# A routed feed-forward kernel: x loaded turned for the router, and the matrices of conditioning by one gather

## The chip, the cores and the metric

One core of a Trainium2 chip runs the whole program. TensorE (PE) multiplies, VectorE (DVE) and ScalarE (ACT) work on its results, GpSimd (POOL) issues the gathers and scatters that go by a list of rows, and SyncE (SP) issues the other DMAs. The metric is device microseconds for one execution; less is better.

## The reference, cut to what matters

```python
w = weights[conditions]                      # 32 of 200 matrices, 64 x 64
xf = einsum('bct,bcd->bdt', x, w)            # x: 32 x 64 x 512; conditioning
logits = einsum('nh,eh->ne', xf, Wr)         # 2048 tokens, 8 experts
gate = softmax(logits); top2 = top_k(gate, 2)
rank = (cumsum(onehot) * onehot).sum(-1); keep = rank <= 640
y = sum over the two experts of gate * Wd(silu(Wg xf) * (Wu xf))
return x + y
```

## The kernel before

The 32 samples are 16 tiles of 128 rows of x (two samples of 64 channels each), eight pairs of tiles in all. Logits don't wait for conditioning: the router's weights are applied to x itself, and each sample's small result is then multiplied by that sample's 64 x 64 matrix (`logits`). For this TensorE turns each tile of x (`x_tile_turn`, L1176), ACT or DVE copies the turned tile out of PSUM (`turn_copy` L810 and L600), `router` (L1188) multiplies it, and `turn` (L1199) turns its small result back. `condition` (L1232) multiplies x by the matrices, two tiles at a time in a ring of four PSUM banks; ACT copies every result (`xf_copy`, L592) and SP stores it to `xf_dram` (L390, L394), from where experts gather their tokens.

The matrices reach `wq` in two ways: tiles 0 to 7 by one row gather each on POOL (L453), tiles 8 to 15 by one gather into `wsel_sb` (L446) and eight placing DMAs of 32 KB on SP's queue (L361), which turn 16 partitions of whole pieces into 128 partitions of rows.

After the logits DVE finds the top two, `oh` is filled, TensorE counts ranks (L1267, L1270), DVE works out the slot of every token (L901 to L929), TensorE makes the lists from it (L1281), and DVE writes `src_row` (L950). POOL then gathers the first expert's tokens into `xg` (L507), for which it waits for `src_row` and for all stores of `xf_dram`. Meanwhile TensorE runs `KEEP_WARM` multiplications whose result nobody reads (L1287). The first use of `xg` is the turn at L1301; from there on the experts run one after the other.

Each engine's order is the order of the code of its block, and an instruction that waits holds all those behind it on its engine. The DMAs of SP start in SP's order. `raw` is the buffer of an expert's weights (five units: four of gate and up, one of down), `w` their split into a high part (ACT, `w_high`) and a low part (DVE, `w0_low`).

Of the kernel before, what the change touches and what calls it, by code (L numbers as in the profile page):

```python
# [22 lines left out]
PLACED = B // 2  # L23
CQ = P // PLACED
# [15 lines left out]
BEFORE_RANKS = 4  # L40
W0_EARLY = 1
LG = ((0, 3), (3, 5), (5, 7), (7, NM))
GATED = 2 * LG[1][1]
EARLY_PAIRS = 2
WARM_UP = 10

KEEP_WARM = 18
# [24 lines left out]
def build(nc, x, cond, wcond, wr, wgu, wd, out):  # L72
# [12 lines left out]
    with ctx:  # L85
# [25 lines left out]
        condb = sb("condb", [P, HALF + 1], I32)  # L111
        row_i = sb("row_i", [P, 1], I32)
        part_i = sb("part_i", [P, 2], I32)
        part = sb("part", [P, 2])
        cidx = sb("cidx", [P, HALF + 1], U32)
# [68 lines left out]
        ps_tT = ps_xf = bank[0:XR]  # L184
# [20 lines left out]
        row_in = [sem(f"row_in{g}") for g in range(len(LG) - 1)]  # L205
        placed = [sem(f"placed{g}") for g in range(1, len(LG))]
        tT_ps = sem("tT_ps")
        tT_act_ok = sem("tT_act_ok")
        tT_dve_ok = sem("tT_dve_ok")
# [69 lines left out]
        TURN_DVE = [1, 2, 5, 6, 9]  # L279
        TURN_ACT = [j for j in range(TT) if j not in TURN_DVE]  # L280

# [61 lines left out]
        def _(sp):  # L343

            def load_x(m):

                js = slice(m * 2, m * 2 + 2)
                sp.dma_start(x_sb[:, js, :], x_t[:, js, :]).then_inc(x_in[m], 16)

            sp.dma_start(condb[:, :], cond[:, :]).then_inc(cond_in, 16)  # L350
            load_x(0)
            load_x(1)
            sp.dma_start(wr_sb[:, :, :], wr[:, :, :]).then_inc(wr_in, 16)
            for m in range(2, NM):
                load_x(m)
# [3 lines left out]
            def place(j):  # L359

                sp.dma_start(wq[:, j, :], wsel_sb[(j - HALF) * 2 * CQ:(j - HALF + 1) * 2 * CQ, :]  # L361
                             .rearrange("q (c d) -> q c d", d=D)).then_inc(placed[group_of(j) - 1], 16)

            sp.wait_ge(wsel_in, 16)
            for j in range(HALF, TT):
                place(j)
# [25 lines left out]
            for j in range(TT - 2, TT):  # L392
                sp.wait_ge(xf_ok, j + 1)
                sp.dma_start(xf_t[:, j:j + 1, :], xf_sb[:, j:j + 1, :]).then_inc(xf_out, 16)  # L394
            sp.wait_ge(gates_ok, 2)
# [39 lines left out]
        def _(pool):  # L435
# [9 lines left out]
            pool.wait_ge(cidx_ok, 2)  # L445
# [3 lines left out]
                in_offset=bass.IndirectOffsetOnAxis(ap=cidx[:, HALF:HALF + 1], axis=0),  # L449
            ).then_inc(wsel_in, 16)  # L450

            for j in range(HALF):
                nc.gpsimd.indirect_dma_start(  # L453
                    out=wq[:, j, :], out_offset=None, in_=wcond[:, :],
                    in_offset=bass.IndirectOffsetOnAxis(ap=cidx[:, j:j + 1], axis=0),
                ).then_inc(row_in[group_of(j)], 16)
# [28 lines left out]
            pool.wait_ge(xf_out, 16 * (TT // 2 + 2))  # L485
# [102 lines left out]
        def _(act):  # L588
            def xf_copy(n, s):

                act.wait_ge(xf_ps, n + 1)
                nc.scalar.activation(xf_sb[:, bass.ds(n, 1), 0:H], ps_xf[s][:, :].unsqueeze(1),  # L592
                                     ACT.Copy).then_inc(xf_ok, 1)

            for j in TURN_ACT:
                act.wait_ge(tT_ps, j + 1)
                if j >= XR:
                    act.wait_ge(xrT_ps, j // 2 - 1)
                nc.scalar.activation(turned_sb[:, j % XR, :, :],  # L600
                                     ps_tT[j % XR][:, :].rearrange("p (k c) -> p k c", k=KH),
                                     ACT.Copy).then_inc(tT_act_ok, 1)
# [12 lines left out]
            def exps(h):  # L615

                act.wait_ge(sub_ok, (1, 3)[h])
                js = (slice(0, GATED), slice(GATED, TT))[h]
                nc.scalar.activation(ex[:, js, :], lg[:, js, :], ACT.Exp).then_inc(ex_ok, 1)

            for n in range(2):
                xf_copy(n, n)
            exps(0)
            for n in range(2, XR):
                xf_copy(n, n)
            for u in range(W0_EARLY):
                w_high(u, 0, 0)
            for n in range(XR, XR + 2):
                xf_copy(n, n - XR)
            exps(1)  # L630
            for n in range(XR + 2, 2 * XR):
                xf_copy(n, n - XR)
            with act.Fori(2, TT // XR) as i:
                for s in range(XR):
                    xf_copy(i * XR + s, s)

            for u in range(W0_EARLY, KH):
                w_high(u, 0, 0)
# [121 lines left out]

            act.wait_ge(consts, IDENT)
            nc.scalar.activation(g_sb[:, 0:1], ident[:, 0:1], ACT.Silu).then_inc(silu_warm, 1)
            w_high(KH, 0, 0)
            x_high(0)
            act.wait_ge(silu_warm, 1)
            act.wait_ge(more_ok, 1)
# [807 lines left out]
```

## Time and profile before

| what | us |
|---|---|
| median of 3 runs (272.05 to 273.76) | 272.7 |
| the profiled execution | 271.69 |
| its span, first to last instruction | 270.0 |
| first turn of a gathered token tile (L1301) starts | 41.62 |
| last `xf_copy` ends | 33.17 |

The span leaves out 1.7 us of the profiled execution. All that the change touches lies ahead of 41.62 us and in the first expert; the other seven experts take the rest of the span. Start times below are from the span's start. An issue of a DMA is shown as an instruction of its queue (SPq, POOL); the landing is given apart.

### The profile page before, as it was taken

The numbers are of one execution on the slowest core, as the hardware profiler recorded it, in microseconds if no ns is written. First come the engines' busy times: TensorE is split into PE (matmuls) and PEld (weight loads), VectorE is DVE, ScalarE is ACT, GpSimd is POOL, SyncE is SP. The second block draws the span as 40 slices with busy tenths as digits, with TensorE's granted clock in tenths as the row PEclk, the third lists the DMA queues.
The fourth block names the chain that finished last, engine by engine and source line by source line (L and its number), as shares of the span: only waits on it lengthen the run. The fifth ranks groups of instructions, "written<-read, shape, count | busy, mean of one in ns | idle before, by whom it ended". The sixth has DMA issues, their size and how long they took to land.

```text
span 270.0 us, 4016 instructions
## 1 busy us (share of the span) xinstructions
PE 257.5 (95%) x1368; PEld 199.9 (74%) x1368; DVE 161.8 (60%) x332; ACT 137.6 (51%) x242; POOL 171.2 (63%) x156
## 2 busy tenths in 40 slices
PE   8999798999999999999999999999999999999991
PEld 4563257999987867888878877887878777778980
DVE  2558997544459674776556638656773967243251
ACT  2356861444464655665376644666475368442100
POOL 5792047731158858875788387768876885585742
PEclk9999979999999999999999999999999999999998
DMA  6999848998879997899789867997899799366541
GB/s 203 364 305 342 358 165 266 382 330 312 298 221 214 203 253 197 138 253 276 178 143 231 245 189 124 241 322 174 171 266 298 127 182 216 41 79 81 146 164 45
DMA packets 27099, 59.00 MB, mean 219 GB/s; under 512 B 6198, under 2 KB 6454, under 8 KB 26976
## 3 DMA queue, kind: packets, MB, share of 16 engines
q1 hardware_dynamic: 16416, 37.89, 44.3%
q0 software_dynamic: 10656, 20.75, 37.2%
q8 instruction: 16, 0.26, 0.4%
q14 instruction: 11, 0.09, 0.1%
HBM read 39.56 MB, written 20.25 MB: 222 GB/s over the span
## 4 chain that ended last, share of the span: by engine, by line
PE 55%; DVE 18%; DMA 9%; ACT 8%; issue 6%; SPq 1%; ACTq 1%; POOLq 0%; DVEq 0%
PE bank L1340 16%; PE bank L1427 10%; PE bank L1314 10%; DMA xg<-xf_dram,src_turn 6%; PE bank L1435 5%; DVE w L996 4%; DVE squares L1045 4%; ACT hhi L695 3%; DMA x_sb<-x 3%; PE bank L1287 2%; PE bank L1301 2%; PE bank L1176 2%; DVE xlo L981 2%; ACT w L608 2%; DVE h L1111 1%
## 5 line engine op out<-in xcount | busy, mean ns | idle before, releaser
L1427 PE MATMUL bank<-xhi,w 128*128 128x512 f32 x280 | 71.5, 397 | 0.2 <-DVE h_last L1091 0.2
L1340 PE MATMUL bank<-w,hhi 128*128 128x512 f32 (+1 forms) x216 | 67.1, 392 | 1.1 <-DVE hlo L1051 1.1
L553 POOL DMA_INDIRECT out<-y_sb,dst_row x35 | 56.1, 1604 | 14.8 <-issue 10.4
L1427 PEld LDWEIGHTS bank<-xhi,w 128*128 128x128 f32 x280 | 52.5, 188 | 13.2 <-DVE h_last L1091 0.7
L519 POOL DMA_INDIRECT gate_g<-gates_dram,src_row x40 | 45.2, 1130 | 12.1 <-issue 10.5
L1340 PEld LDWEIGHTS bank<-w,hhi 128*128 128x128 f32 x216 | 39.2, 188 | 10.2 <-DVE hlo L1051 2.3
L996 DVE TENSOR_TENSOR w<-raw,w 128x704 fp32r<-128x704 f32 (+1 forms) x35 | 37.0, 1058 | 14.6 <-ACT w L608 8.2
L1340 PE MATMUL bank<-w,hlo 128*128 128x512 f32 (+1 forms) x108 | 42.0, 389 | 0.0
L507 POOL DMA_INDIRECT xg<-xf_dram,src_turn x24 | 25.5, 1063 | 26.1 <-DVE xlo L981 11.7
L1435 PE MATMUL bank<-xlo,w 128*128 128x512 f32 x140 | 38.4, 396 | 0.0
L608 ACT ACTIVATE w<-raw 128x704 fp32r<-128x704 f32 (+1 forms) x40 | 36.7, 922 | 0.0
L507 POOL DMA_INDIRECT xg<-xf_dram,src_row x16 | 17.6, 1102 | 27.9 <-DVE dst_row L965 15.7
L1045 DVE STREAM_TRANSPOSE squares<-xg 128x512 f32<-128x512 f32 x24 | 24.0, 1051 | 16.7 <-DMA xg<-xf_dram,src_turn 16.7
L1435 PEld LDWEIGHTS bank<-xlo,w 128*128 128x128 f32 x140 | 26.4, 188 | 6.4
L666 ACT ACTIVATE y_sb<-bank,gate_g 128x512 f32<-128x512 f32 x30 | 20.1, 685 | 20.0 <-PE bank L1340 18.7
L1340 PEld LDWEIGHTS bank<-w,hlo 128*128 128x128 f32 x108 | 20.3, 188 | 4.7
L1314 PE MATMUL bank<-w,xhi 128*128 128x352 f32 x112 | 20.5, 328 | 0.8 <-ACT xhi L643 0.8
L1314 PEld LDWEIGHTS bank<-w,xhi 128*128 128x128 f32 x112 | 18.2, 189 | 1.5 <-issue 1.0
L695 ACT ACTIVATE hhi<-h 128x512 fp32r<-128x512 f32 x14 | 8.8, 632 | 19.5 <-DVE h L1098 12.0
L1051 DVE TENSOR_TENSOR hlo<-h,hhi 128x512 fp32r<-128x512 f32 x14 | 9.7, 696 | 10.4 <-ACT hhi L695 10.4
L981 DVE TENSOR_TENSOR xlo<-xg,xhi 128x512 fp32r<-128x512 f32 x24 | 15.0, 685 | 0.2 <-ACT xhi L653 0.2
L653 ACT ACTIVATE xhi<-xg 128x512 fp32r<-128x512 f32 x24 | 13.2, 617 | 1.5 <-DMA xg<-squares 1.5
(138 smaller groups left out, 304.3 us busy)
## 6 DMA issues: line engine op xcount, KB each, us to landing
raw<-wgu SPq DMA_DIRECT2D x32, 352.0 KB, 7.7
xg<-squares SPq DMA_DIRECT2D x24, 256.0 KB, 7.1
x_sb<-x SPq DMA_DIRECT2D x8, 512.0 KB, 8.3
raw<-wd SPq DMA_DIRECT2D x8, 512.0 KB
xf_dram<-xf_sb SPq DMA_DIRECT2D x7, 512.0 KB, 3.7
raw<-wd SPq DMA_DIRECT2D x8, 192.0 KB
out<-x SPq DMA_DIRECT2D x1, 1280.0 KB, 17.9
gate_g<-gates_dram,src_row POOLq DMA_INDIRECT x40, 4.5
```

The source lines that it names most:

```text
L507: nc.gpsimd.indirect_dma_start(out=xg[:, t, :], out_offset=None, in_=xf_dram[:, :], in_offset=bass.IndirectOffsetOnAxis(ap=rows, axis=0), ...
L519: nc.gpsimd.indirect_dma_start(out=gate_g[:, n % TPE, :], out_offset=None, in_=gates_dram[:, :], in_offset=bass.IndirectOffsetOnAxis(ap=sr ...
L553: nc.gpsimd.indirect_dma_start(out=out[:, :], in_=y_sb[:, n % TPE, :], in_offset=None, out_offset=bass.IndirectOffsetOnAxis(ap=dst_row[:, ...
L608: last = nc.scalar.activation(w[:, half, 0, a:b], raw[:, a:b], ACT.Copy)
L666: nc.scalar.activation(y_sb[:, t, :], y_bank(e, t)[:, :], ACT.Copy, scale=gate_g[:, t, e:e + 1]).then_inc(y_ok, n)
L981: nc.vector.tensor_tensor(xlo4[:, :, cols], turned_rows(e, t), xhi4[:, :, cols].bitcast(F32), ALU.subtract).then_inc(xlo_ok, n)
L996: last = nc.vector.tensor_tensor(w[:, half, 1, a:b], raw[:, a:b], w[:, half, 0, a:b].bitcast(F32), ALU.subtract)
L1045: nc.vector.transpose(squares[:, :, t, :], xg[:, t, :].rearrange("p (i b) -> p b i", i=SQ)).then_inc(squares_ok, 1)
L1314: last = nc.tensor.matmul(ps[:, 0:I], left[:, b, c], w[:, half, part, o:o + I], start=(k == 0 and left is xhi and part == 0), stop=(k == K ...
L1340: last = nc.tensor.matmul(ps[:, cols], left(c), w[:, half, part, o:o + width], start=(c == 0 and q == 0), stop=(closes and c == cs[-1] and ...
L1427: last = nc.tensor.matmul(ACC_BANK[what][:, :], columns(what, k, part), xhi4[:, k, :], start=(k == 0 and part == 0), stop=False)
L1435: last = nc.tensor.matmul(ACC_BANK[what][:, :], columns(what, k, 0), xlo4[:, k, :], start=False, stop=(k == KH - 1))
```

## The change

Outside the kernel a second copy of x, `xt`, is made in which every pair of tiles is turned. SP loads it into the place of x (`x_sb`), 4 KB for a partition where rows were two pieces of 2 KB. `router` reads it at once: 16 tile turns and their 16 copies on ACT and DVE are gone. Conditioning needs the rows: for pairs 0, 1 and 2 SP loads them over the turned ones, once the router has read these (`load_x_rows`); for pairs 3 to 7 TensorE turns the tiles back (`turn_rows`) and ACT copies them to `x_sb` (`rows_copy`). Pairs are conditioned in the order 3, 4, 0, 1, 2, 5, 6, 7, with two places in the ring. One gather of 128 rows of 4 KB now fetches all 32 matrices, and ACT issues 16 placing DMAs, each from 8 partitions, ahead of all its other work. Exponentials and gates are worked out once for all tiles and no longer in two parts. Units 2 to 4 of the first expert's weights are loaded after the stores of `xf_dram`; `x_low(0)` now stands ahead of `w0_low(KH)`; `KEEP_WARM` goes from 18 to 28.

```diff
-PLACED = B // 2
-CQ = P // PLACED
+CQ = P // B
-W0_EARLY = 1
+W0_EARLY = 2
+ROWS_LOADED = (0, 1, 2)
+ROWS_TURNED = (3, 4, 5, 6, 7)
+CONDITIONED = (3, 4, 0, 1, 2, 5, 6, 7)
-KEEP_WARM = 18
+KEEP_WARM = 28
 SP:
+            def load_x_turned(m):
+                sp.dma_start(x_sb[:, m * 2:m * 2 + 2, :], xt[m, :, :, :]).then_inc(x_in[m], 16)
+            def load_x_rows(n):
+                m = ROWS_LOADED[n]
+                sp.wait_ge(xrT_ps, m + 1)
+                sp.dma_start(x_sb[:, js, :], x_t[:, js, :]).then_inc(rows_in[n], 16)
-            sp.wait_ge(wsel_in, 16)
-            for j in range(HALF, TT):
-                place(j)
+            for n in range(len(ROWS_LOADED)):
+                load_x_rows(n)
...
-            for u in range(NU):
+            for u in range(W0_EARLY):
                 load_unit(0, u)
-            for m in range(NM - 1):
-                sp.wait_ge(xf_ok, m * 2 + 2)
+            for n, m in enumerate(CONDITIONED):
+                sp.wait_ge(xf_ok, n * 2 + 2)
...
+            for u in range(W0_EARLY, NU):
+                load_unit(0, u)
 POOL:
-            for j in range(HALF):
-                nc.gpsimd.indirect_dma_start(
-                    out=wq[:, j, :], out_offset=None, in_=wcond[:, :],
...
 ACT:
+            act.wait_ge(wsel_in, 16)
+            for j in range(TT):
+                act.dma_start(wq[:, j, :], wsel_sb[j * 2 * CQ:(j + 1) * 2 * CQ, :]
+                              .rearrange("q (c d) -> q c d", d=D)).then_inc(placed[group_of(j)], 16)
+            def rows_copy(m, ring):
+                for o in range(2):
+                    act.wait_ge(turned_ps, ROWS_TURNED.index(m) * 2 + o + 1)
+                    nc.scalar.activation(x_sb[:, m * 2 + o, :], ps_xf[ring * 2 + o][:, :],
+                                         ACT.Copy).then_inc(turned_ok, 1)
 PE:
-            def x_tile_turn(j):
...
+            def turn_rows(m, ring):
+                for o in range(2):
+                    for k in range(KH):
+                        last = nc.tensor.transpose(ps_xf[ring * 2 + o][:, k * P:(k + 1) * P],
+                                                   xt_sb[:, m * 2 + o, k, :], ident[:, :])
+                    last.then_inc(turned_ps, 1)
+            def condition(m, ring):
...
+                if m in ROWS_LOADED:
+                    pe.wait_ge(rows_in[ROWS_LOADED.index(m)], 16)
+                else:
+                    pe.wait_ge(turned_ok, ROWS_TURNED.index(m) * 2 + 2)
```

On ACT, from its first instruction: before, it loads its table, copies turned tiles and then results of conditioning (`xf_sb`).

```order
L600 ACT_TABLE_LOAD
L600 ACTIVATE turned_sb<-bank 128x512 [waits tT_ps] x2
L600 ACTIVATE turned_sb<-bank 128x512 [waits xrT_ps,tT_ps] x9
L592 ACTIVATE xf_sb<-bank 128x512 [waits xf_ps] x2
L619 ACTIVATE ex<-lg 128x80 [waits sub_ok]
L592 ACTIVATE xf_sb<-bank 128x512 [waits xf_ps] x2
L608 ACTIVATE w<-raw 128x704 [waits raw_in0]
```

On ACT from its first instruction in the changed kernel (`x_sb` are the rows turned back; `wsel_in` counts the landed gather):

```order
L577 DMA wq<-xf_sb 128x1x64 [waits wsel_in]
L577 DMA wq<-xf_sb 128x1x64 x15
L591 ACT_TABLE_LOAD
L591 ACTIVATE x_sb<-bank 128x512 [waits turned_ps] x4
L584 ACTIVATE xf_sb<-bank 128x512 [waits xf_ps]
L584 ACTIVATE xf_sb<-bank 128x512
L584 ACTIVATE xf_sb<-bank 128x512 [waits xf_ps]
L584 ACTIVATE xf_sb<-bank 128x512
L591 ACTIVATE x_sb<-bank 128x512 [waits turned_ps] x4
```

The sixteen placings, the wait for the gather ahead of them and the table load behind them now stand before every copy.

On TensorE around the last router step, before: L1221 are logits, L1232 conditioning, L1188 the router, L1199 its turn, L1267 and L1270 the ranks.

```order
L1221 MATMUL bank_5<-xr,wq 64x8 x8
L1232 MATMUL bank<-x_sb,wq 64x512 x4
L1188 MATMUL bank_7<-turned_sb,wr_sb 32x256 x4
L1199 MATMUL bank_7<-ident,xrT 128x128 x2
L1232 MATMUL bank<-x_sb,wq 64x512 x4
L1199 MATMUL bank_7<-ident,xrT 128x128 x2
L1221 MATMUL bank_5<-xr,wq 64x8 x8
L1221 MATMUL bank_7<-xr,wq 64x8 x4
L1232 MATMUL bank<-x_sb,wq 64x512 x8
L1267 MATMUL bank_7<-ohp,ones 128x264
```

The same place of TensorE in the changed kernel (L1167 logits, L1182 conditioning, L1130 the router, L1150 its turn, L1140 turning rows back, L1220 the ranks):

```order
L1167 MATMUL bank_5<-xr,wq 64x8 x8
L1182 MATMUL bank<-x_sb,wq 64x512 x4
L1130 MATMUL bank_7<-x_sb,wr_sb 32x256 x4
L1150 MATMUL bank_7<-ident,xrT 128x128 x4
L1167 MATMUL bank_5<-xr,wq 64x8 x8
L1167 MATMUL bank_7<-xr,wq 64x8 x4
L1182 MATMUL bank<-x_sb,wq 64x512 x4
L1140 MATMUL bank<-ident,x_sb 128x128 x16
L1220 MATMUL bank_7<-ohp,ones 128x264
```

The first conditioning, of pair 3, still stands ahead of the last router step, but now it waits for ACT's copies of the rows; two pairs of tiles are turned back ahead of the ranks.

## Rows read from the trace of the kernel before

**Rows 1.** The chain that ended last, in order of time: start us, us, what

```profile
33.43 2.55 PE bank L1281 x32
35.98 5.58 PE bank L1287 x18
...
41.62 0.64 PE bank L1301 x4
```

**Rows 2.** Timeline of POOL, then the landing of DMAs issued from 37 to 39

```profile
37.46 1.55 POOL L507 DMA_INDIRECT xg<-xf_dram,src_row  x1 [15.70 <-DVE dst_row L965]
...
xg<-xf_dram,src_row POOLq DMA_INDIRECT x1, 4.0
```

**Rows 3.** Timeline of SP and its DMA issues from 0 to 50: KB, median us to landing

```profile
10.87 5.14 SPq L361 DMA_DIRECT2D wq<-xf_sb  x8
...
32.71 1.32 SPq L394 DMA_DIRECT2D xf_dram<-xf_sb  x2
...
xf_dram<-xf_sb SPq DMA_DIRECT2D x7, 512.0 KB, 3.7
...
xf_dram<-xf_sb SPq DMA_DIRECT2D x2, 256.0 KB, 3.4
```

**Rows 4.** Timeline of DVE, 34.9 to 50.5

```profile
36.02 0.20 DVE L950 TENSOR_SCALAR src_row<-bank 128x40 uint32<-128x40 f32 x1
...
43.52 3.58 DVE L1144 COPY src_turn<-src_row 32x6 uint32<-32x6 uint32 x16
47.14 0.69 DVE L974 TENSOR_TENSOR xlo<-bank,xhi 128x512 fp32r<-128x512 f32 x1
```

**Rows 5.** Timeline of ACT, 20 to 52

```profile
24.75 0.79 ACT L608 ACTIVATE w<-raw 128x704 fp32r<-128x704 f32 x1
...
26.86 1.09 ACT L592 ACTIVATE xf_sb<-bank 128x512 f32<-128x512 f32 x2
...
31.11 2.06 ACT L592 ACTIVATE xf_sb<-bank 128x512 f32 x4 [0.32 <-PE bank L1232]
...
35.24 1.28 ACT L762 ACT_TABLE_LOAD   x1
```

**Rows 6.** The gathering queue, 8 to 9 and 9 to 10 us: packets, MB, share

```profile
q0 software_dynamic: 21, 0.09, 23.6%
...
q0 software_dynamic: 71, 0.19, 50.9%
```

**Rows 7.** Timeline of TensorE, 18 to 30, and one step of the first expert

```profile
18.47 1.09 PE L1176 MATMUL bank<-ident,x_sb 128*128 128x128 f32 x8
...
20.69 1.07 PE L1232 MATMUL bank<-x_sb,wq 64*64 64x512 f32 x8
21.69 0.64 PE L1188 MATMUL bank<-turned_sb,wr_sb 128*32 128x256 f32 x8
...
24.01 0.78 PE L1221 MATMUL bank<-xr,wq 64*64 64x8 f32 x24
...
48.71 0.80 PE L1314 MATMUL bank<-w,xlo 128*128 128x352 f32 x4
```

**Rows 8.** Stretches: busy us (instructions) of PE, PEld, DVE, ACT, POOL; PEclk, DMA share, GB/s

```profile
30.00:33.40 3.40, 1.93 (x16) 0.27 (x13) 3.23 (x10) 3.08 (x7) 0.00 (x0) 1.00 0.90 361
...
36.00:39.40 3.40, 3.40 (x9) 1.18 (x8) 3.27 (x11) 2.10 (x3) 1.64 (x2) 0.50 0.08 22
39.40:41.60 2.20, 2.16 (x10) 0.79 (x9) 2.00 (x2) 0.00 (x0) 1.90 (x2) 1.00 0.54 145
```

**Rows 9.** By tile (raw) and line: ns min/median/max of one, first and last start us

```profile
L372 SPq DMA_DIRECT2D raw<-wgu x8: 333/432/587, 16.1 to 42.9; - x8
...
L941 DVE TENSOR_TENSOR w<-raw,w x5: 873/885/1753, 35.1 to 39.6; 128x704 fp32r<-128x704 f32 x4, 128x1536 fp32r<-128x1536 f32 x1
```

**Rows 10.** DMAs issued from 43 to 43.5, and packets from 15.9 to 18.2

```profile
xg<-xf_dram,src_row POOLq DMA_INDIRECT x1, 7.0
...
DMA packets 1323, 0.48 MB, mean 209 GB/s; under 512 B 1232, under 2 KB 1232, under 8 KB 1323
```

More of the change, by code:

```diff
@@ L204, in build @@
         wsel_in = sem("wsel_in")
[L205 to L209, printed above, removed]
+        placed = [sem(f"placed{g}") for g in range(len(LG))]
+        rows_in = [sem(f"rows_in{m}") for m in ROWS_LOADED]
+        turned_ps = sem("turned_ps")
+        turned_ok = sem("turned_ok")
         xrT_ps = sem("xrT_ps")
@@ L613, in w_high, with exps @@
                 last.then_inc(whi_ok, 1)
[L615 to L637, printed above, removed]
+            def exps():
+                act.wait_ge(sub_ok, 2)
+                nc.scalar.activation(ex[:, :, :], lg[:, :, :], ACT.Exp).then_inc(ex_ok, 1)
+            rows_copy(3, 0)
+            rows_copy(4, 1)
+            xf_copy(3, 0)
+            xf_copy(4, 1)
+            rows_copy(5, 0)
+            rows_copy(6, 1)
+            xf_copy(0, 0)
+            xf_copy(1, 1)
+            rows_copy(7, 0)
+            xf_copy(2, 1)
+            exps()
+            xf_copy(5, 0)
+            xf_copy(6, 1)
+            w_high(0, 0, 0)
+            xf_copy(7, 0)
+            for u in range(1, KH):
                 w_high(u, 0, 0)
@@ L942, in w0_low @@
                                         ALU.subtract).then_inc(wlo0_ok, 1)
-            for u in range(W0_EARLY):
-                w0_low(u)
+            gates()
             dve.wait_ge(slot_ps, 1)
@@ L966, in _ @@
                                     ALU.add).then_inc(lists_ok, 1)
-            for u in range(W0_EARLY, KH):
+            for u in range(KH):
                 w0_low(u)
@@ L1240, in _ @@
             pe.wait_ge(consts, IDENT)
-            for m in range(NM):
-                x_tile_turn(m * 2)
-                x_tile_turn(m * 2 + 1)
-                if m == 1:
-                    pe.wait_ge(wr_in, 16)
-                if m >= 1:
-                    router(m - 1)
-                if m >= 2:
-                    turn(m - 2)
-                if m in (6, 7):
-                    logits(m - 6)
-            condition(0)
+            pe.wait_ge(wr_in, 16)
+            for m in range(NM - 1):
+                router(m)
+                if m >= 1:
+                    turn(m - 1)
+                if m == 3:
+                    turn_rows(3, 0)
+                if m == 4:
+                    turn_rows(4, 1)
+                if m in (5, 6):
+                    logits(m - 5)
+            pe.wait_ge(turned_ok, 2)
+            condition(3, 0)
             router(NM - 1)
             turn(NM - 2)
-            condition(2)
             turn(NM - 1)
@@ L1258, in _ @@
             logits(3)
-            after = EARLY_PAIRS * 2 + BEFORE_RANKS
-            for j in range(EARLY_PAIRS * 2, after, 2):
-                condition(j)
+            pe.wait_ge(turned_ok, 4)
+            condition(4, 1)
+            pe.wait_ge(xf_ok, 2)
+            turn_rows(5, 0)
+            pe.wait_ge(xf_ok, 4)
+            turn_rows(6, 1)
             pe.wait_ge(consts, RANKS)
@@ L1272, in _ @@
             last.then_inc(rank_ps, 1)
-            for j in range(after, TT, 2):
-                condition(j)
+            pe.wait_ge(turned_ok, 6)
+            condition(0, 0)
+            pe.wait_ge(turned_ok, 8)
+            condition(1, 1)
+            pe.wait_ge(xf_ok, 6)
+            turn_rows(7, 0)
+            pe.wait_ge(xf_ok, 8)
+            condition(2, 1)
+            pe.wait_ge(turned_ok, 10)
+            condition(5, 0)
+            pe.wait_ge(xf_ok, 10)
+            condition(6, 1)
+            pe.wait_ge(xf_ok, 12)
+            condition(7, 0)
             pe.wait_ge(consts, CONSTS)
```

164 lines of the change are left out of this document (52 added, 112 removed).

## The prediction

> **What bounds the kernel now.** I read the chain of waits first, up to the first turn of a gathered tile. It runs through the multiplication that makes the lists, through 18 fillers, and into that turn at 41.62 [rows 1]. The fillers hide two things that end together. One is on POOL: the gather into `xg` is issued at 37.46 and lands 4.0 us later, at 41.5 [rows 2], while the fillers end at 41.56. So the turn waits for the gather, and I asked what the gather waits for. `src_row` is there at 36.2 [rows 4]; the last two stores of `xf_dram` are issued from 32.7 to 34.0 and land 3.4 us after their issue starts, so the later one at about 37 [rows 3]. The list is ready more than 1 us before the gather starts: the stores set the start, and behind them stands ACT, whose last copy of a result ends at 33.17 [rows 5]. From this copy to the turn it takes 8.4 us. So the question for the change is when ACT makes its last copy, and whether the lists stay ahead of it.
>
> **What goes away.** Sixteen tile turns on TensorE and sixteen copies, and on POOL eight row gathers, on SP eight placings (5.14 us) [rows 3]. All of this lies ahead of the last router step at 21.69 [rows 7], and it is worth only as much as that step and the conditioning behind it come sooner. In the changed order neither can: conditioning of pair 3 stands ahead of the last router step on TensorE and waits for ACT's copies of the rows.
>
> **When ACT begins.** ACT's first instruction waits for the gather of the matrices. Before, SP began to place at 10.87, when a gather of 256 KB had landed [rows 3]; its queue moved little until 9 us and then 0.19 MB in a microsecond, half of the DMA engines [rows 6]. Twice the bytes at that rate take 1.4 us more: 12.2. Bounds are 10.5 (nothing more, indices a little earlier) and 14.4 (bytes and competition both double the stretch from 8.6). Then sixteen issues. The trace has none on ACT. The nearest row is the same transfer of 32 KB on SP's queue, 5.14 us for eight, 0.643 each [rows 3]; the shortest DMA issue of its kind is 0.333 [rows 9]. I take SP's: 10.3 us, ACT is through at 22.5. The lower bound is 5.0 us less. Then ACT loads its table, 1.28 us [rows 5], which before was hidden at the start: 23.8.
>
> **ACT's work from there.** It has 26 copies in place of 16: ten of rows, sixteen of results, at 0.545 us (two in 1.09), 14.2 us; one exponential, 0.27; the high part of weight unit 0 ahead of the last pair, 0.79 [rows 5]. That is 15.2. To this come waits. Rows of pair 3 are copied at 24.9, TensorE conditions it by 25.95 (1.07) [rows 7], and then does the last router step, its turns and the logits. Before, that took 3.1 us from 21.69 to 24.79 with one conditioning in between, which covered 0.4 us of DVE's work; without it, 2.4 [rows 7]. So logits end at 28.4 and pair 4 is conditioned at 29.4, while ACT had finished pair 3 at 27.1: it waits 2.3 us. Pair 0 comes after two pairs are turned back (1.06 each, 1.09 in the row) [rows 7] and after the ranks: ACT waits another 0.5. After that ACT doesn't wait. 23.8 + 15.2 + 2.9, with 0.1 of hops, is 42.0 for the last copy, against 33.17.
>
> **From the last copy to the turn.** The last store, now 512 KB, lands 3.6 us after its issue (median 3.7) [rows 3]: 45.6. A gather of 4.0 [rows 2] from 45.7 lands at 49.7. But units 2 to 4 of the weights, 1.4 MB, now stand right behind the last store on SP's queue. A gather beside such loads took 7.0 instead of 4.0 [rows 10]; this one meets only their end, and I add 1.0 (bounds 0 and 3): 50.7. TensorE's side: the lists come after the last conditioning, at 40.1, and end at 42.65 (2.55) [rows 1]. Eighteen fillers took 5.6 us, nine of them in 3.4 us at a granted 0.50, which is 1.2 GHz, the others at 0.216 each at full clock [rows 8]; ten more are 2.2, so 28 end at 50.5. The turn starts at 50.7, 9.1 later than before. The late units themselves are off the path: units 2 and 3, 0.7 MB right behind a store that lands at 45.6, land at 48 to 49 at the rate of that store, and ACT's and DVE's parts of them (0.79 and 0.88) [rows 5, 9] end before the second half of the first expert's first step needs them. If that cover goes, it costs up to 1 us.
>
> **The clock.** The granted clock fell to 0.50 at 36 after a stretch in which TensorE was busy 1.93 of 3.4 us, and stayed there for 3.4 us of fillers [rows 8]. While ACT places, TensorE has nothing but a few small logits from about 17 to 25, so I expect the low clock when pair 3 begins. Its conditioning, the router step, turns and logits, 3.1 us of work on the path, would then take up to 1.7 us more. I take 0.8.
>
> **DVE in the first expert.** `x_low(0)` now comes ahead of `w0_low(KH)`, which can start only when ACT has made the high part behind its first copy, and the sixteen copies of `src_turn` stand behind that. From the turn: 2.8 us until the high part is there, 1.75 [rows 9], 3.58 [rows 4], so the second `xlo` starts after 8.15 and ends after 8.85, where before it started after 5.5 (47.14) [rows 4]. TensorE needs it 7.1 us after the turn (48.71) [rows 7]. So 1.75 us of a new stall, and nothing hides it.
>
> **The sum.** 9.1 + 0.8 + 1.75 = 11.65 us on the profiled execution's 271.7, that is 283.3. The median of the runs lies 1.0 above that execution, so I forecast 284.3, given as 284. The POOL time set free, exponentials and gates in one piece (counted with ACT, or beside waiting on DVE) and 4 KB pieces for x are worth nothing: none is on this path.
>
> **Rivals.** (1) *ACT's issues are short.* If one holds ACT only 0.333 us [rows 9], everything from ACT's start comes 5.0 us sooner: 279.3. For it: some loads on SP are issued in as little. Against: the same transfer took 0.592 at the least on SP, which the eight in 5.14 us bear out. (2) *The placings run on half of the engines.* Before, a placing read 16 partitions and now it reads 8. In the trace 1232 small packets took most of 2.3 us [rows 10], so the 1024 of eight placings some 1.9. If the number of source partitions sets the number of engines, twice the packets on half of the engines occupy these for 7.6 us; with half of their time [rows 6] the last matrix lands about 28, just when logits want it; with a third, about 35, 7 us late. The middle costs 3.5 to 4 us, since logits stand ahead of all other conditioning on TensorE: 288. It decides from a landing after 28.4. The trace can't speak for it, since no placing of before reads fewer than 16 partitions. The Trainium skill has this as a rule (DMA: Bandwidth & Descriptors, section "Why a DMA increments its semaphore by 16 and not by 1"): a DMA is spread over the largest number of engines, up to 16, that divides the slowest dimension of both of its sides, which would be 8 here; no run here shows it. (3) *Not slower.* The last copy would have to end at 33.17 less the 1.75 of DVE's stall. ACT's work and waits behind the table load are 18.2 us, so that load would have to end by 13.2, and the gather land and sixteen issues pass by 11.9. That needs the gather at about 10.5 and issues that hold ACT hardly at all (0.1 us each, under any row). For it: ACT is shown issuing nothing, so its price isn't known. Then the last copy comes at 33.5, the weights' 1.0 falls away with the wait, and the time is 272 to 274.
>
> **How the numbers follow.** The forecast gets 0.70, (1) 0.12, (2) 0.11, (3) 0.07. The low end of the range joins both low bounds of ACT's start (5.0 and 1.7): 284.3 - 6.7, 278. The high end: the gather at 14.4 (2.2), the full 7.0 of the token gather (2.0), the whole clock loss (0.9): 289.4, which holds (2) as well. A measurement of this kernel can tell about 1%, 2.7 us. Of (3) I count 0.05 as within 1% and 0.02 as faster; all other cases are slower by over 1%.
>
> **What would show it.** In the changed profile: sixteen placings on ACT's queue of about 0.64 us each from about 12.2, then a table load and the first copy to `x_sb` near 24; the last conditioning copy near 42; the first `xg` gather near 46; the turn near 51 to 52; a second `xlo` 8 us behind the turn. A first copy before 18 would make me wrong by rival (1); logits that wait for the placings after 28, by (2).

## The result, and the profile after

The changed kernel takes 289.3 us (median; 287.6 to 292.1), the kernel before 273.2 on the same chip: a ratio of 1.0574, with a 95% interval of 1.0505 to 1.0642. It is slower, as forecast, 5 us beyond the forecast of 284 and just inside the range, whose upper end is 289.4. Ratios (not medians) leave out executions more than 1.5% above the fastest of the same kernel, and the profiled executions of "old matrices", "38 fillers", "both" and "rows on DVE" are such ones, so for these I read where waits stand rather than the total, and "both", with one execution left, has no ratio.

The profiled execution took 287.6 us, the least of the four, 15.9 more than that of before. First the chain of waits of the changed kernel, from the last placings to the first turn of a gathered tile (start us, us, what):

```profile
24.68 0.61 ACTq L577
...
25.32 1.28 ACT L591
26.61 1.09 ACT x_sb L591 x2
...
27.84 1.99 PE bank L1182 x8
29.83 1.05 PE bank L1130 x8
...
32.79 0.96 PE bank L1182 x8
...
33.78 1.10 ACT xf_sb L584 x2
...
44.81 0.98 ACT xf_sb L584 x2
45.81 2.97 DMA xf_dram<-xf_sb
...
49.55 5.07 DMA xg<-xf_dram,src_row
...
54.76 1.06 PE bank L1266 x4
```

Before, this stretch of the chain was TensorE's lists and fillers up to a turn at 41.62 [rows 1]. Now it begins with ACT's DMA issues, goes through its table load and its first copies of rows, the conditioning of pair 3, the last router step and, by turns, ACT's copies and TensorE's turning and conditioning to the last store, and ends in a turn at 54.76, 13.1 us later. ACT, on its own timeline, places, and much later makes its last copy of a result, which ends at 45.78 in place of 33.17 [rows 5]:

```profile
12.82 12.47 ACTq L577 DMA_DIRECT2D wq<-xf_sb  x16
...
33.78 1.09 ACT L584 ACTIVATE xf_sb<-bank 128x512 f32<-128x512 f32 x2 [2.81 <-PE bank L1182]
...
44.69 1.09 ACT L584 ACTIVATE xf_sb<-bank 128x512 f32<-128x512 f32 x2
```

TensorE's timeline shows who else waits for the placings (first line), that the fillers end at 52.72, 2.03 us before the turn, and what follows from this in the first expert:

```profile
23.66 0.53 PE L1167 MATMUL bank<-xr,wq 64*64 64x8 f32 x24 [4.53 <-DMA wq<-xf_sb]
...
46.50 6.22 PE L1252 MATMUL bank<-iota_q 128*128 128x512 f16 x28
54.76 1.04 PE L1266 MATMUL bank<-ident,xg 128*128 128x128 f32 x4 [2.03 <-DMA xg<-xf_dram,src_row]
56.58 2.69 PE L1279 MATMUL bank<-w,xhi 128*128 128x352 f32 x8 [0.78 <-ACT xhi L631]
...
64.58 0.81 PE L1279 MATMUL bank<-w,xlo 128*128 128x352 f32 x4
65.23 0.49 PE L1333 MATMUL bank<-ident,h_sb 128*128 128x128 f32 x3
```

The stretches of the same execution (busy us of PE, PEld, DVE, ACT and POOL; then the granted clock, DMA share and GB/s) tell why eight multiplications take 2.69 us, where the same eight took 1.53 before: the clock is at 0.50, which is 1.2 GHz, after the wait of 2.03 us. It is there from 25 to 30 as well, after the wait of 4.53:

```profile
25.00:30.00 5.00, 3.59 (x34) 1.37 (x34) 2.39 (x25) 3.46 (x6) 0.00 (x0) 0.50 0.11 17
30.00:35.00 5.00, 4.35 (x53) 2.09 (x46) 3.29 (x25) 2.19 (x5) 0.00 (x0) 0.91 0.26 107
...
55.00:60.00 5.00, 4.22 (x16) 3.85 (x15) 2.82 (x5) 1.97 (x2) 4.24 (x4) 0.50 0.88 293
```

From the turn to the first turn of h (line 1333) it took 10.47 us; in the trace before it took 7.73. So the 15.9 us are 13.14 up to the turn and 2.74 behind it; the rest of the kernel adds nothing. DVE's timeline answers to [rows 4]:

```profile
57.84 1.76 DVE L906 TENSOR_TENSOR w<-raw,w 128x1536 fp32r<-128x1536 f32 x1 [0.68 <-ACT w L598]
59.52 3.39 DVE L1106 COPY src_turn<-src_row 32x6 uint32<-32x6 uint32 x16
62.94 0.69 DVE L936 TENSOR_TENSOR xlo<-bank,xhi 128x512 fp32r<-128x512 f32 x1
```

The second `xlo` starts 8.18 us behind the turn, forecast as 8.15. Yet TensorE reaches its use only at 64.58, when `xlo` has been there since 63.6: after half clock TensorE is later than DVE here.

Last, the queues. q1 is SP's, q10 ACT's placings. From 17 to 21 and from 22 to 24 us (packets, MB, share of 16 engines):

```profile
q1 hardware_dynamic: 703, 1.45, 97.3%
q10 hardware_dynamic: 336, 0.08, 9.4%
...
q10 hardware_dynamic: 1029, 0.25, 57.0%
q1 hardware_dynamic: 19, 0.04, 6.4%
```

While SP's queue still loads rows and weights, the placings get 84 packets of 256 bytes in a microsecond; once it is through they get 514, and then 57% of the engines' time.

### The profile page after: what moved, and what is told of

It reads as the page before. It is cut to its first block, busy times and chain, and to the rows that moved or that the text cites. A ratio compares the mean times of both kernels' runs of the same rounds, so it can differ in the third digit from the quotient of the medians.

```text
span 285.9 us, 3939 instructions
## 1 busy us (share of the span) xinstructions
PE 264.0 (92%) x1354; PEld 202.3 (71%) x1354; DVE 158.1 (55%) x321; ACT 136.4 (48%) x240; POOL 168.0 (59%) x148
## 4 chain that ended last, share of the span: by engine, by line
PE 59%; DMA 14%; DVE 9%; ACT 6%; ACTq 4%; issue 4%; SPq 1%; POOL 1%; POOLq 1%; DVEq 0%
PE bank L1305 18%; PE bank L1394 15%; PE bank L1279 10%; PE bank L1402 7%; ACTq L577 4%; DMA xg<-xf_dram,src_turn 4%; DMA xf_sb<-wcond,cidx 3%; DMA xg<-squares 3%; DVE w L958 3%; DVE squares L1007 3%; PE bank L1182 2%; PE bank L1266 2%; ACT xf_sb L584 2%; DMA xg<-xf_dram,src_row 2%; PE bank L1409 1%
## 5 line engine op out<-in xcount | busy, mean ns | idle before, releaser
L539 POOL DMA_INDIRECT out<-y_sb,dst_row x35 | 57.4, 1640 | 14.6 <-issue 10.4
L505 POOL DMA_INDIRECT gate_g<-gates_dram,src_row x40 | 48.0, 1200 | 12.1 <-issue 11.2
L493 POOL DMA_INDIRECT xg<-xf_dram,src_turn x24 | 26.0, 1082 | 24.6 <-DVE xlo L943 9.9
L654 ACT ACTIVATE y_sb<-bank,gate_g 128x512 f32<-128x512 f32 x30 | 20.2, 686 | 20.0 <-PE bank L1305 18.6
L1279 PE MATMUL bank<-w,xhi 128*128 128x352 f32 x112 | 22.0, 344 | 0.8 <-ACT xhi L631 0.8
L1279 PEld LDWEIGHTS bank<-w,xhi 128*128 128x128 f32 x112 | 19.6, 202 | 1.6 <-issue 1.1
L1013 DVE TENSOR_TENSOR hlo<-h,hhi 128x512 fp32r<-128x512 f32 x14 | 9.7, 692 | 10.4 <-ACT hhi L683 10.4
```

The lines of the kernel that those rows point to most:

```text
L493: nc.gpsimd.indirect_dma_start(out=xg[:, t, :], out_offset=None, in_=xf_dram[:, :], in_offset=bass.IndirectOffsetOnAxis(ap=rows, axis=0), ...
L505: nc.gpsimd.indirect_dma_start(out=gate_g[:, n % TPE, :], out_offset=None, in_=gates_dram[:, :], in_offset=bass.IndirectOffsetOnAxis(ap=sr ...
L539: nc.gpsimd.indirect_dma_start(out=out[:, :], in_=y_sb[:, n % TPE, :], in_offset=None, out_offset=bass.IndirectOffsetOnAxis(ap=dst_row[:, ...
L654: nc.scalar.activation(y_sb[:, t, :], y_bank(e, t)[:, :], ACT.Copy, scale=gate_g[:, t, e:e + 1]).then_inc(y_ok, n)
L1279: last = nc.tensor.matmul(ps[:, 0:I], left[:, b, c], w[:, half, part, o:o + I], start=(k == 0 and left is xhi and part == 0), stop=(k == K ...
```

## The experiments

Each is the changed kernel with one edit. Ratios are to the kernel before on the same chip. The last four columns are of the profiled execution (us): ACT's first copy, the end of the last copy of a result, the first turn of a gathered tile, and from there to the turn of h.

| kernel | median | ratio to before | first copy | last copy ends | turn | to turn of h |
|---|---|---|---|---|---|---|
| before | 272.6 to 273.2, by chip | 1 | | 33.17 | 41.62 | 7.73 |
| after | 289.3 | 1.0574 [1.0505, 1.0642] | 26.61 | 45.78 | 54.76 | 10.47 |
| placings on SP | 282.0 | 1.0327 [1.0273, 1.0381] | 13.84 | 38.09 | 48.35 | 9.28 |
| rows after placing | 286.9 | 1.0526 [1.0490, 1.0563] | 25.02 | 47.23 | 56.51 | 9.27 |
| sixteen partitions | 286.1 | 1.0517 [1.0426, 1.0608] | 22.73 | 44.37 | 52.48 | 9.27 |
| table first | 290.6 | 1.0636 [1.0570, 1.0703] | 26.24 | 47.08 | 56.07 | 10.43 |
| rows on DVE | 289.4 | 1.0521 [1.0433, 1.0609] | 29.62 | 48.40 | 57.81 | 9.26 |
| list early | 289.2 | 1.0626 [1.0540, 1.0712] | 26.68 | 47.48 | 55.63 | 9.21 |
| 38 fillers | 289.2 | 1.0583 [1.0517, 1.0649] | 27.50 | 48.53 | 57.91 | 9.27 |
| both | 289.6 | none | 27.53 | 48.74 | 57.71 | 7.79 |
| clock held | 291.0 | 1.0633 [1.0544, 1.0722] | 27.36 | 47.52 | 56.97 | 10.45 |
| old matrices | 281.4 | 1.0259 [1.0183, 1.0334] | 12.29 | 40.22 | 49.06 | 9.30 |
| old matrices, mended | 279.3 | 1.0236 [1.0193, 1.0278] | 13.17 | 40.63 | 49.44 | 7.73 |
| on SP, mended | 280.6 | 1.0320 [1.0266, 1.0375] | 14.71 | 38.36 | 48.95 | 7.74 |

**Placings on SP.** The five lines move from ACT to SP, ahead of the loads of rows:

```diff
 # sync
+            sp.wait_ge(wsel_in, 16)
+            for j in range(TT):
+                sp.dma_start(wq[:, j, :], wsel_sb[...]...).then_inc(placed[group_of(j)], 16)
             for n in range(len(ROWS_LOADED)):
                 load_x_rows(n)
 # scalar
-            act.wait_ge(wsel_in, 16)
-            for j in range(TT):
-                act.dma_start(wq[:, j, :], wsel_sb[...]...).then_inc(placed[group_of(j)], 16)
```

> The changed kernel with its 16 placings issued by SP, ahead of the row loads, in place of ACT. Theory (ACT is held by the wait for the gather, 16 issues and a table load, 12.8 to 26.6): the table load falls back to the start, ACT copies the rows of pair 3 by 17, and conditioning of pair 3 waits only for the matrices, about 22.5 in place of 27.84; logits end at 26 to 27 in place of 32.8; the last copy comes near 41 in place of 45.8, the first turn near 50 in place of 54.76; the time is 4 to 5.5 us under the changed kernel's, a ratio to the kernel before of 1.037 to 1.043. Rival A (ACT's 26 copies and the ring of two places are the cost, not its late start): last copy within 1.5 of 45.8, ratio 1.052 or more. Rival B (placings from 8 partitions run on half of the engines and are what the logits wait for): logits still end after 30.

The direction is the theory's, and the gain is larger than it forecast: pair 3 is conditioned at 21.1, logits end at 25.1, and the ratio of 1.0327 lies below the expected 1.037 to 1.043, which its interval just reaches. Neither rival's sign shows: the last copy is 7.7 us earlier, and the logits end well before 30. SP's timeline, then ACT's and POOL's:

```profile
12.44 10.42 SPq L361 DMA_DIRECT2D wq<-xf_sb  x16
...
13.84 0.60 ACT L591 ACTIVATE x_sb<-bank 128x512 f32<-128x512 f32 x1 [11.74 <-PE bank L1140]
...
44.08 1.00 POOL L498 DMA_INDIRECT xg<-xf_dram,src_row  x1 [32.25 <-DMA xf_dram<-xf_sb]
```

ACT starts 12.8 us sooner and ends 7.7 us sooner. The gather starts 6.0 us behind the last copy, where it was 3.8 in the changed kernel: the rows and weights, now behind the placings, share the queues with the stores (the DMA engines are full from 30 to 45, by a share of 1.01 to 1.03, where the changed kernel has 0.26 to 0.85). The edit does two things at once: it frees ACT, and it keeps SP's loads from competing with the placings. So it doesn't rule out rival B for the changed kernel. The next run does the second alone.

**Rows after placing.**

```diff
+            sp.wait_ge(placed[3], 32)
             for n in range(len(ROWS_LOADED)):
                 load_x_rows(n)
```

> SP waits for the last placing before it issues the rows of pairs 0 to 2 and the first two weight units, which are not needed before about 30 us. Theory (ACT's issues are stretched because its queue gets only 8 to 10% of the engines' time beside SP's loads and backs up): x turned is through near 17, the placings run alone from there, the sixteen issues take 10 to 11 us in place of 12.5, the first copy comes near 24 in place of 26.6, and the run is 2 to 3 us shorter than the changed kernel: ratio 1.046 to 1.050. Rival (the length of an issue has nothing to do with SP's loads): first copy again at 26 to 27, ratio 1.057. A cost that could show: the rows meet the stores.

ACT's timeline, then two steps of TensorE's:

```profile
12.88 10.82 ACTq L578 DMA_DIRECT2D wq<-xf_sb  x16
23.73 1.28 ACT L592 ACT_TABLE_LOAD   x1 [23.73 <-issue]
25.02 2.06 ACT L592 ACTIVATE x_sb<-bank 128x512 f32<-128x512 f32 x4
...
21.75 0.41 PE L1168 MATMUL bank<-xr,wq 64*64 64x8 f32 x16 [1.09 <-DMA wq<-xf_sb]
26.25 1.99 PE L1183 MATMUL bank<-x_sb,wq 64*64 64x512 f32 x8 [4.08 <-ACT x_sb L592]
```

With SP's queue through at about 16 us the sixteen issues take 10.82 us in place of 12.47, and in the changed kernel's other variants up to 13.8. So an issue's length depends on what the other queue moves. TensorE's two lines show what ACT's late start costs by itself: the matrices come early, the logits that stand ahead of pair 3 are through by 22.2, and pair 3 still waits 4.08 us for ACT's copies. The total doesn't show a gain: 2.4 us by medians, 1.3 by the ratios, whose intervals overlap, and in the profiled execution the last copy came 1.5 us later than in the changed kernel's, at a clock of 0.50 from 25 to 35. So the 7.3 us between the placings on ACT and on SP can't be split into a share of ACT's and a share of the competition.

**Sixteen partitions.** The gather is made in two pieces, as it was in width before, so that each placing reads 16 partitions:

```diff
-            nc.gpsimd.indirect_dma_start(out=wsel_sb[:, :], ..., ap=cidx[:, :] ...).then_inc(wsel_in, 16)
+            for h in range(2):
+                nc.gpsimd.indirect_dma_start(out=wsel_sb[:, h * CP * D:(h + 1) * CP * D], ...,
+                    ap=cidx[:, h:h + 1] ...).then_inc(wsel_in[h], 16)
...
-                act.dma_start(wq[:, j, :], wsel_sb[j * 2 * CQ:(j + 1) * 2 * CQ, :]
+                if j % HALF == 0:
+                    act.wait_ge(wsel_in[j // HALF], 16)
+                q, c = j % HALF * 2 * CQ, j // HALF * CP * D
+                act.dma_start(wq[:, j, :], wsel_sb[q:q + 2 * CQ, c:c + CP * D]
```

> The changed kernel with the gather of 512 KB cut in two of 256 KB, so that each of the 16 placings on ACT reads 16 partitions and not 8; same bytes, same number of small packets, same queue. If the number of source partitions sets the number of engines (rival B), the last placings move at about twice the packets a microsecond (1000 in place of 521 in the stretch from 22 to 23), the long issues on ACT (0.83, 1.03, 1.61) go, ACT is through near 23 in place of 25.3, and the time falls by about 2 us, ratio near 1.050. If the long issues and late landings come from the other queue's loads alone, packets a microsecond and issues stay as they are, ratio 1.055 to 1.060.

The median is what was expected, but the interval covers both forecasts. The first copy comes 3.9 us sooner, and 2.5 of these are another effect of the edit: ACT starts at 10.29, since the first half of the gather lands sooner; the issues take 11.12 in place of 12.47. The mechanism shows in the queues. From 16 to 20 us, and from 22 to 22.25, when SP's queue is nearly through and the placings still queue:

```profile
q1 hardware_dynamic: 693, 1.36, 88.0%
q10 hardware_dynamic: 692, 0.16, 18.6%
...
q10 hardware_dynamic: 267, 0.06, 113.6%
q1 hardware_dynamic: 6, 0.01, 9.6%
```

**Table first.** A copy of one column ahead of the placings makes ACT load its table early:

```diff
+            act.wait_ge(consts, IDENT)
+            nc.scalar.activation(g_sb[:, 0:1], ident[:, 0:1], ACT.Copy)
             act.wait_ge(wsel_in, 16)
```

> The changed kernel with one copy of a single column ahead of ACT's wait for the gather, so that its table is loaded at the start. Theory (ACT's start is on the path, one for one): first copy of rows near 25.3 in place of 26.61, everything up to the turn 1.3 us earlier, ratio about 1.053. If pair 3 were waiting for its matrices or its transposes and not for ACT: nothing moves, ratio 1.057.

A miss. The load moved out of the way (the first copy starts 0.05 us after the last issue, where it was 1.32), but the sixteen issues took 13.71 us, the first copy came only 0.4 us sooner, and the clock stayed at 0.50 from 25 to 35. What the table load costs in total time stays open.

**Rows on DVE.** DVE copies pairs 3 and 4 while ACT places:

```diff
-            rows_copy(3, 0)
-            rows_copy(4, 1)
             xf_copy(3, 0)
 # vector, in the loop over pairs
+                if m in (4, 5):
+                    for o in range(2):
+                        n = (m - 4) * 2 + o
+                        dve.wait_ge(turned_ps, n + 1)
+                        nc.vector.tensor_copy(x_sb[:, 6 + n, :], ps_xf[n][:, :]).then_inc(turned_ok, 1)
```

> DVE copies the rows of pairs 3 and 4 while ACT still places; ACT then starts with the results of pair 3. Theory (conditioning of pair 3, and with it the last router step, waits for ACT's copies of rows): TensorE conditions pair 3 at about 24 in place of 29, logits end with the last placing near 28 to 29 in place of 32.8, ACT makes 22 copies and no longer waits 2.8 us, the last copy ends at 41.5 to 42.5 in place of 45.8 and the run is 3 to 4 us shorter: ratio 1.043 to 1.047. Rival (the matrices, placed on half of the engines, hold the logits nearly as long as ACT does): at most 1.5 us shorter, ratio 1.052 or more.

The interval covers both forecasts. TensorE's timeline speaks for the rival:

```profile
24.63 0.82 PE L1171 MATMUL bank<-xr,wq 64*64 64x8 f32 x24 [6.78 <-DMA wq<-xf_sb]
...
27.56 2.00 PE L1186 MATMUL bank<-x_sb,wq 64*64 64x512 f32 x8
```

Nothing waits for ACT's copies any more, and yet pair 3 is conditioned at 27.56, against 27.84: the matrices of the first group come at 24.6. In the changed kernel ACT held this step only 1.35 us longer than the matrices and the logits behind them did. So two waits end there side by side, ACT's copies and the matrices. "Rows after placing" takes the second away and leaves 4.08 us of the first, this run takes the first away and leaves the second; only the placings on SP shorten both.

**The first expert: list early, 38 fillers, both.** In the first the copies of `src_turn` stand ahead of `x_low(0)` and `w0_low(KH)` on DVE; in the second KEEP_WARM is 38; the third does both.

```diff
+            ... the sixteen copies to src_turn ...
             x_low(0)
             w0_low(KH)
-            ... the sixteen copies to src_turn ...
...
-KEEP_WARM = 28
+KEEP_WARM = 38
```

> The changed kernel with the 16 copies of src_turn ahead of x_low(0), in DVE's idle time before the first turn. Theory (the stall that the prediction put on DVE in the first expert, 1.75 us, is there, but lies behind a larger one: the fillers end 2 us before the gather lands, the clock falls, and the first expert begins at half speed): the second xlo comes some 3 us sooner, and from the first turn of a gathered tile to the first turn of h it still takes about 10.4 us as in the changed kernel (7.7 before); ratio unchanged, 1.054 to 1.060. Rival (DVE's order is what the first expert waits for): that stretch falls to about 8.7, ratio 1.050.

> The changed kernel with 38 fillers in place of 28, so that they end near 54.9, with the gather's landing. Theory: TensorE's clock stays at full, the first expert's steps run at full speed, and DVE's order now shows: from the first turn to the first turn of h about 9.5 us (7.7 and the 1.75 of the prediction); a gain of about 0.9 less 0.2 of lateness, ratio about 1.055. Rival (the clock alone): that stretch falls to 7.8, gain 2.5, ratio 1.048.

> The changed kernel with both: src_turn early and 38 fillers. Theory: from the first turn to the first turn of h 7.7 to 8.0 us as before, 2.5 us less than in the changed kernel, ratio about 1.048. If either rival of the other two runs holds alone, this run adds nothing to the better of them.

The four stretches from turn to turn of h make a square: 10.47 with neither, 9.21 with the list early (at a clock of 0.69 from 55 to 60), 9.27 with more fillers, 7.79 with both, against 7.73 before. "List early" fits neither of its forecasts (10.4 and 8.7); the other two fit their theories by this stretch. The corner with neither is not one number: "clock held" and "table first" have 10.45 and 10.43, but five other executions with neither mend have 9.26 to 9.30. In these the second `xlo` ends just ahead of its use, as here in "rows after placing" (DVE, then TensorE):

```profile
64.28 0.69 DVE L937 TENSOR_TENSOR xlo<-bank,xhi 128x512 fp32r<-128x512 f32 x1
...
65.13 0.81 PE L1280 MATMUL bank<-w,xlo 128*128 128x352 f32 x4
```

So there DVE's order sets the stage, and in the changed kernel's profiled execution the clock, 1.2 us later. Either one alone costs about 1.5 us, and only both mends bring the stage back. With 38 fillers the clock stays at 1.00 from 55 to 65, and DVE's stall appears on TensorE's timeline:

```profile
66.43 0.91 PE L1279 MATMUL bank<-w,xlo 128*128 128x352 f32 x4 [1.30 <-DVE xlo L936]
```

The totals don't show these gains. In these profiled executions the last copy came 1.7 to 3.0 us later than in the one of the changed kernel, at a clock of 0.50 where that had 0.91 (30 to 35); TensorE's waits behind 90 us, in the later experts, came to 2.2 to 4.1 us against 1.4.

**Clock held.** 32 fillers on TensorE before the first logits and 10 before pair 3 is conditioned:

```diff
+                if m == 5:
+                    filler(32, 4)
                 if m in (5, 6):
                     logits(m - 5)
+            pe.wait_ge(xrT_ok, NM - 1)
+            filler(10, 6)
             pe.wait_ge(turned_ok, 2)
```

> The changed kernel with 32 fillers of 256 columns ahead of TensorE's wait for the first matrices and 10 ahead of its wait for the rows of pair 3, into parts of banks that nobody reads. Theory (the low clock after the wait costs up to 1.7 us of the path, the term that the prediction took at 0.8): granted clock 1.00 from 25 to 30 where it was 0.50, conditioning of pair 3 takes 1.07 in place of 1.99, from the first copy of rows to the last copy of conditioning 17.5 in place of 19.2, ratio about 1.051. If the clock does not matter there, the stretch stays at 19.

A miss of the edit, not a test of the theory: the 32 ended at 21.86, TensorE waited 2.51 us, the clock was 0.62 from 25 to 30, and the ten ran at half clock (2.32 us) in front of pair 3.

**Old matrices.** Eight row gathers on POOL and eight placings on SP ahead of the rows, as before the change; all else as changed:

```diff
+            for j in range(HALF):
+                nc.gpsimd.indirect_dma_start(out=wq[:, j, :], ..., in_=wcond[:, :], ...).then_inc(row_in[group_of(j)], 16)
...
+            for j in range(HALF, TT):
+                sp.dma_start(wq[:, j, :], wsel_sb[...]...).then_inc(placed[group_of(j) - 1], 16)
...
-            for j in range(TT):
-                act.dma_start(wq[:, j, :], wsel_sb[...]...).then_inc(placed[group_of(j)], 16)
```

> The changed kernel with the matrices as before: 8 row gathers on POOL, one gather of 256 KB and 8 placings from 16 partitions on SP, ahead of the row loads. What is left of the change is the turned load, the rows loaded or turned back, and the order. Theory: ACT is free from the start, pair 3 is conditioned near 20, logits end near 23, the last copy comes 13 us later, near 36 (45.8 - 32.8 in the changed kernel), the turn near 45; ratio 1.015 to 1.025: two thirds of the loss lies in how the matrices come, one third in the ten more copies and the first expert. Rival A: last copy still beyond 42, ratio over 1.045. If the turned load alone were a gain, the ratio would be under 1.00.

The interval reaches into what was expected, but the last copy ended only at 40.2, 4 us later than forecast (and short of rival A's 42). The granted clock was 0.52 and 0.50 from 20 to 30.

**Old matrices, mended; on SP, mended.** The last two ask whether a version of the change is as fast as the kernel before. Both have the list early; the first has 36 fillers, the second, with sixteen placings on SP, 42.

```diff
-KEEP_WARM = 28
+KEEP_WARM = 36      (42 with the placings on SP)
```

> Matrices as before the change (eight row gathers on POOL, eight placings on SP), list of turned tiles early, 36 fillers: what the turned load alone costs when the rest is put right. Theory (ten more copies on ACT, 5.5 us, lie on the path to the last store, whatever the matrices do): last copy at 38 to 40, turn near 48.5, first expert 7.8 from turn to turn of h: ratio 1.010 to 1.020. Rival (the old matrices and the early list undo it all): ratio 1.000 to 1.005.

> One gather and sixteen placings as in the change, but issued on SP, list of turned tiles early, 42 fillers. Theory: as with the placings on SP (ratio 1.033), less 1.3 us for the list and up to 2 us for the clock in the first expert: ratio 1.020 to 1.026, and 0 to 1% above the version with the old matrices.

Both have the first expert back (7.73 and 7.74), and neither comes near the kernel before: 1.0236 and 1.0320, both a little above what I expected. The turned load keeps the last copy 5.2 to 7.5 us later, whichever way the matrices come. POOL's first gather of tokens with the old matrices:

```profile
44.35 1.01 POOL L505 DMA_INDIRECT xg<-xf_dram,src_row  x1 [22.71 <-DMA xf_dram<-xf_sb]
```

and with the placings on SP:

```profile
44.71 1.01 POOL L498 DMA_INDIRECT xg<-xf_dram,src_row  x1 [32.87 <-DMA xf_dram<-xf_sb]
```

The first had its last copy at 40.63, at a clock of 0.50 from 25 to 30; the second, at a clock of 1.00 from 20 on, at 38.36, but its gather started 6.4 us behind that in place of 3.7. What one gains the other loses. ACT's first two copies of results with the old matrices, mended, then the first of the kernel before:

```profile
21.83 1.08 ACT L591 ACTIVATE xf_sb<-bank 128x512 f32<-128x512 f32 x2 [5.76 <-PE bank L1201]
27.21 1.09 ACT L591 ACTIVATE xf_sb<-bank 128x512 f32<-128x512 f32 x2 [4.29 <-PE bank L1201]
...
21.82 1.08 ACT L592 ACTIVATE xf_sb<-bank 128x512 f32<-128x512 f32 x2 [1.57 <-PE bank L1232]
```

The first result is copied at the same time in both, so all that the turned load saves ahead of it gains nothing, and the 7.5 us arise behind it. The fastest kernel that I ran remains the one before.

## Why the prediction was right, and where its sizes were off

The direction and the mechanism held: ACT, made to issue the placings, starts its copies late, and from its last copy on all of the delay reaches the turn. By the steps of the sum:

- **When ACT begins.** The gather let ACT start at 12.8 (forecast 12.2). The sixteen issues took 12.47 us, not 10.3; this is the term that was mis-sized most. The price of one was right, 0.612 in the median on ACT and 0.604 on SP; but four took 0.8 to 1.6. In the run with the rows held back the first still took 1.21 and no other was long: the other three, 1.6 us beyond the median, come with SP's loads beside them. The table load was 1.28 as in the rows. First copy 26.6, forecast 23.8: 2.8 us. The upper bound for the gather, 14.4, doesn't follow from the stretch that it names: doubling the 2.27 us from 8.6 to 10.87 gives 13.1, doubling them twice 17.7. The range's upper end holds 2.2 us for that bound, so that 289.3 lies just inside is partly luck.
- **ACT's work from there**, with the clock's 0.8: 19.0 forecast, 19.17 measured. That the sum fits is partly luck. ACT waited 4.9 us in this stretch (1.21, 2.81, 0.60, 0.27) for the 2.9 forecast and the 0.8 of the clock, and its own work took 14.3 for 15.2. In the other executions with the placings on ACT the stretch took 20 to 22 us, with the clock at half speed for longer. Full clock and half clock are to be seen side by side: conditioning a pair took 1.09 at 1.00 (pair 4, at 32.63) and 1.99 at 0.50 (pair 3, at 27.84).
- **From the last copy to the turn**: 8.7 forecast, 8.98 measured; the last store took 2.97 for 3.6, the gather 5.07 for 5.0 beside the late weights, and POOL 0.73 for its issue.
- **The fillers.** I forecast that they end 0.2 us before the turn. They ended 2.03 us before it, mostly because I gave the 28 of them 7.85 us, nine at half clock as in [rows 8], and they ran at full clock in 6.22. Then the clock fell. This term was not in the sum. It cost the first expert 2.7 us, and took the place of the next one.
- **DVE in the first expert.** The order of DVE was right to 0.03 us, but the 1.75 of a stall was not what this execution waited for. It is there when the clock is held (9.27 less 7.73 is 1.54) and in the five executions of the experiments with 9.26 to 9.30. So the prediction had a right cause that a larger one covered here, and both have to be mended to get the stage back.

The sum of what was off is 2.8 + 0.2 + 0.3 up to the turn and 1.0 behind it, 4.3 us: 283.3 on the profiled execution became 287.6.

Of the rivals, short issues fell at once (0.61 at the least). Not slower fell with them. Placings on half of the engines is true as a mechanism, by the packet counts, and came nearer than I had it: I let it decide from a landing after 28.4 with half of the engines' time, and the last packets moved before 27; but the first group already came 4.5 us after TensorE asked for it, while beside SP's loads the placings had 9% of the engines' time and not half. ACT ended only 1.35 us behind the logits that this held, so that the main chain of the prediction held by a narrow margin.

What the parts of the change cost: the placings on ACT in place of SP 7.3 us by medians (6.7 by the ratios, whose intervals are apart); the one gather with sixteen placings in place of the old matrices, both mended, 1.3 by medians and 2.3 by the ratios, whose intervals overlap slightly, so this is not clear of noise; all that is left of the change in "old matrices, mended" 6.6 (279.3 less 272.7). For this last part the traces show where the 7.5 us lie by which the last copy comes later, all of them between the first copy of a result and the last. Six of the ten copies of rows stand there, 3.3 us of work (the other four are made by 16.1, while ACT has nothing else to do). The other 4.2 are longer waits for TensorE, 6.2 in place of 2.0; the longest is for pair 4, behind the last router step and the logits, 4.29 us at a clock of 0.50 and 2.58 at 1.00 in "on SP, mended". No run puts back by itself the order of the pairs, the gates in two parts or the early weights: what each costs in time stays open. So does why the clock came back by 35 us in one execution of the changed kernel and not in others.

## What to carry to other kernels

A DMA issue is an instruction with a price on the engine that issues it, 0.6 us here and more when another queue is loaded: sixteen of them ahead of an engine's own work delay that work by their sum (12.47 us here), so put them on an engine that nobody waits for. Where two waits end side by side, as ACT's copies and the matrices did here, taking one away gains little; look for the second before counting on the first. When work moves from one engine to another, count what the second has to do before its last needed result; here sixteen turns and copies fewer ahead of the first result gave nothing back, and six copies and longer waits behind it cost 7.5 us. And where fillers are counted to cover a wait, any delay uncovers them: look at the granted clock behind the wait before explaining the next stage by its waits.

## What the chip showed that I had not expected

- In every profiled execution with the placings on ACT the granted clock was at 0.50 to 0.62 from 25 to 30 us, behind waits of TensorE for the matrices or the rows; with the placings on SP it was 0.98 to 1.00 from 20 to 50. From 30 to 35 it was 0.91 in the changed kernel, where first to last copy took 19.2 us, and 0.50 in "both", where it took 21.2.
